# Three more items per tile in split precision, four of the differences on VectorE, and a new order of the engines' work

## The chip, the cores and the metric

The kernel runs on one core of a Trainium2 chip. The metric is the device time of one execution in microseconds (us). The median of three runs of the kernel before is 1046.57 us (1046.28 to 1047.83).

## The reference

The reference is a recommendation tower. Per sample 32 rows of 16 numbers are looked up (one in each of 32 tables), three cross layers follow, and then a small dense network. Batch 1024.

```python
e = jnp.stack([tbl_0[ids[:, 0]], ..., tbl_31[ids[:, 31]]], axis=1)        # (1024, 32, 16)
x0 = h = e
for i in range(3):                                  # W_i has 128 rows, b_i 128
    z = (x0[:, :, None, :] * h[:, None, :, :]).reshape(B, F * G, E)
    y = relu(einsum('oc,bce->boe', W[i], z) + b[i][None, :, None])
    x_keep, h = (y[:, :64], y[:, 64:]) if i != 2 else (y, y)
    xs.append(x_keep)
z = sum(concatenate(xs, axis=1), axis=2)            # (1024, 256)
h = maximum(concatenate([z, dense_ctx], axis=1) @ W_top1 + b_top1, 0)
h = maximum(h @ W_top2 + b_top2, 0)
y = h @ W_top3                                      # (1024, 1)
```

## The kernel before

A block is 128 samples, a tile is one block and 4 of the 16 embedding places: 512 columns. There are 8 blocks, so 32 tiles. A cross layer of a tile is a contraction over pairs of rows: VectorE multiplies a 128-row arrangement of x by h, two chunks of 128 pairs at a time (128x1024 numbers), and TensorE multiplies the chunks by the weights and adds up in PSUM. Such a pair of chunks is an **item**, written (layer, number): (0,0) and (0,1), (1,0) to (1,7), (2,0) to (2,7). Layer 0 has one more, smaller piece, the squares, called TAIL.

An item is multiplied in one of two ways. **Whole**: the product `prod` and the weights are plain fp32, two matmuls. **Split**: ScalarE rounds the product to fp32r (`high`), another engine makes the rest, `unsplit - high` (`low`), and TensorE does three fp32r matmuls per chunk: high by the weights' high part, high by their low part, and low by the high part. Before, 7 of the 8 items of layer 2 are split, 11 items are whole. GpSimd (POOL in the profile) makes all 7 differences, except three in the last slot.

The work is written out by hand as **slots**. Slot s holds layer 0 of tile s+1, layer 1 of tile s and layer 2 of tile s-1; the list `SLOT` gives the items' order, and every engine walks through it and waits on semaphores. Slots go from -1 to 32; those from 2 to 29 are in a loop of four slots. TensorE does the low part of a split item one item later than its high part. Products lie in rings: four for whole items, four for items that POOL finishes, two for VectorE's. A ring's buffer comes free when TensorE has finished the item in it (`s_used`).

Around the items stand, on each engine, in its own order:

- POOL issues the lookups of the next block, eight per slot (each an indirect DMA of 128 rows), and the tail's difference (`split_tail`). The lists `LOOKUPS_AFTER` place them between the differences.
- ScalarE casts `high`, makes h of the next layer from the PSUM sums (`next_h0`, and for h1 at a slot's end), copies the kept halves to SBUF (`keep`), copies the looked-up block into `emb` once per block (`take_rows`, which waits until all 32 lookups have landed), spreads it (`repeat_fields`), and takes the transposed x (`take_x`: a copy that goes to HBM and comes back in two arrangements, and the squares).
- VectorE makes the products, adds the kept halves of a tile to `acc_kept` (`add_kept`), the last layer to `acc_last` (`add_last`), and once per block sums the four places (`fold`).
- SyncE (SP) stores x and loads its arrangements `shifted` (1 MB) and `spread` (four loads of 1 MB) for each tile.

PSUM's eight banks before: y0, y1, two y2, two h0, h1, xT.

Of the kernel before, what the change touches and what calls it, by code (L numbers as in the profile page):

```python
# [30 lines left out]
ALU = mybir.AluOpType  # L31
# [7 lines left out]
P = 128  # L39
# [32 lines left out]
def uses_of_parity(t):  # L72
# [7 lines left out]
SLOT = [(1, 0), (1, 1), (2, 0), (1, 2), (2, 1), (1, 3), (0, 0), (2, 2), TAIL, (1, 4), (0, 1),  # L80
        (2, 3), (1, 5), (2, 4), (1, 6), (2, 5), (1, 7), (2, 6), (2, 7)]
# [3 lines left out]
TURN_AFTER = {-1: (0, 1), 0: (1, 4)}  # L85
# [45 lines left out]
class Plan:  # L133
# [28 lines left out]

    def place(self, s, item, ring):

        kind = self.kind(s, item)
        if isinstance(s[0], int):
            return self.entry(s, item) % ring[kind]
        return (self.before(kind, s[1]) + self.rank(s, item)) % ring[kind]


def dlrm_tower(nc, dense_ctx, ids, tables, w_top1, b_top1, w_top2, b_top2, w_top3,
# [8 lines left out]
    with ExitStack() as ctx:  # L180
# [98 lines left out]
        y2 = [ps(f"y2_{p}", [P, COLS]) for p in range(2)]  # L279
        h0 = [ps(f"h0_{p}", [P, COLS]) for p in range(2)]  # L280
# [3 lines left out]
        prep = [bank[:, :].rearrange("p (a b) -> p a b", b=P) for bank in y2]  # L284
# [50 lines left out]
        s_sum_kept = sem("s_sum_kept")  # L335
# [940 lines left out]
```

## Time and profile before

| | |
|---|---|
| median of 3 runs | 1046.57 us |
| the profiled execution | 1047.29 us |
| its span, first to last instruction | 1045.5 us |
| mean granted TensorE clock | 0.99 |
| busy: TensorE, VectorE, ScalarE, GpSimd | 96%, 74%, 47%, 78% |

The span is 1.8 us shorter than the time of the same execution. Each engine's busy time is a share of the span. A matmul's end is modelled, so what an item costs TensorE is read from where the next one starts, not from its own length.

### The profile page before, as it was taken

To read this page: it belongs to the slowest core of one execution; us is meant where nothing else is said; L and a number is where in the kernel's file an instruction comes from. 1 tells how busy PE (TensorE), PEld (TensorE's weight loads), DVE (VectorE), ACT (ScalarE), POOL (GpSimd) and SP (SyncE) were. 2 spreads that over 40 slices of the span, in tenths; PEclk is the share of its full clock that TensorE was granted. 3 is DMA by queue.
4 is the path that set the end of the run, shared out by engine and by line. 5 is a ranking of instruction groups with operands and counts; after the bars stand their busy time and mean duration, and the time that the engine had idled before them with its cause. 6 is when DMAs were issued, how large, how long until landed. Compare 5 with 4: busy or idle time off the path is not lost.

```text
span 1045.5 us, 11551 instructions
## 1 busy us (share of the span) xinstructions
PE 1007.8 (96%) x3261; PEld 590.5 (56%) x3261; DVE 771.7 (74%) x723; ACT 491.7 (47%) x630; POOL 813.8 (78%) x524
## 2 busy tenths in 40 slices
PE   3889999999999999999999999999999999999988
PEld 3744555555555555555555555555555555555555
DVE  4356787778787777777788777777788777777982
ACT  2153554544444554544444554454444555453443
POOL 6666889887989789887989789888989855556640
PEclk9899999999999999999999999999999999999999
DMA  8099998888998888888898888888897878779000
GB/s 160 8 203 219 204 201 180 180 182 178 198 200 174 189 176 183 181 181 179 193 203 171 192 177 184 181 180 181 190 204 167 198 176 181 177 179 218 16 1 1
DMA packets 42868, 176.27 MB, mean 169 GB/s; under 512 B 15522, under 2 KB 20130, under 8 KB 22372
## 3 DMA queue, kind: packets, MB, share of 16 engines
q1 hardware_dynamic: 34660, 173.96, 75.3%
q0 software_dynamic: 8192, 2.11, 1.9%
q8 instruction: 8, 0.13, 0.1%
q14 instruction: 8, 0.07, 0.0%
HBM read 172.89 MB, written 3.15 MB: 168 GB/s over the span
## 4 chain that ended last, share of the span: by engine, by line
PE 82%; DVE 5%; POOL 3%; DMA 3%; issue 2%; ACT 2%; SPq 2%; POOLq 0%; ACTq 0%; DVEq 0%
PE y L640 51%; PE y L648 17%; PE y L663 9%; POOL low L509 2%; PE xT L600 2%; DVE unsplit L1107 1%; PE xT L612 1%; DMA spread<-xcols 1%; DVE prod L1107 1%; POOL looked_up L499 1%; DMA looked_up<-in_tbl,ids_now 1%; SPq L431 1%; PE y L657 1%; DMA xcols<-xrows 1%; DVE z_kept_low L1184 0%
## 5 line engine op out<-in xcount | busy, mean ns | idle before, releaser
L509 POOL TENSOR_TENSOR low<-unsplit,high 128x1024 fp32r<-128x1024 f32 x221 | 525.1, 2389 | 120.9 <-ACT high L866 118.6
L640 PE MATMUL y<-prod,w1T 128*128 128x512 f32 x1024 | 477.8, 594 | 3.2 <-ACT kept L858 2.1
L1107 DVE TENSOR_TENSOR prod<-spread,h 128x1024 f32<-128x1024 f32 x288 | 349.6, 1216 | 122.4 <-PE y L640 105.4
L866 ACT CAST high<-unsplit 128x1024 fp32r<-128x1024 f32 x224 | 233.9, 1045 | 267.1 <-DVE unsplit L1107 266.9
L1107 DVE TENSOR_TENSOR unsplit<-spread,h 128x1024 f32<-128x1024 f32 x224 | 271.8, 1214 | 84.6 <-ACT h L852 84.6
L499 POOL DMA_INDIRECT looked_up<-in_tbl,ids_now x256 | 246.5, 963 | 66.1 <-issue 56.9
L640 PEld LDWEIGHTS y<-prod,w1T 128*128 128x128 f32 x1024 | 192.4, 190 | 162.5 <-issue 141.2
L648 PE MATMUL y<-high,w2T_high 128*128 128x512 f32 x448 | 226.7, 506 | 4.3 <-ACT high L866 4.3
L663 PE MATMUL y<-low,w2T_high 128*128 128x512 f32 x448 | 202.4, 533 | 2.3 <-POOL low L509 2.0
L648 PE MATMUL y<-high,w2T_low 128*128 128x512 f32 x448 | 177.5, 396 | 0.0
L852 ACT ACTIVATE h<-y,bias 64x512 f32<-64x512 f32 x128 | 83.3, 651 | 169.9 <-PE y L640 169.0
L663 PEld LDWEIGHTS y<-low,w2T_high 128*128 128x128 f32 x448 | 84.3, 190 | 85.7 <-issue 61.5
L640 PE MATMUL y<-prod,w0T 128*128 128x512 f32 x256 | 122.0, 599 | 3.1 <-DVE prod L1107 3.1
L648 PEld LDWEIGHTS y<-high,w2T_high 128*128 128x128 f32 x448 | 84.8, 189 | 49.5 <-issue 29.9
L648 PEld LDWEIGHTS y<-high,w2T_low 128*128 128x128 f32 x448 | 84.7, 189 | 43.5 <-issue 29.2
L1107 DVE TENSOR_TENSOR prod<-shifted,xT 128x1024 f32<-128x1024 f32 x64 | 77.8, 1216 | 16.5 <-DMA shifted<-xcols 6.5
L640 PEld LDWEIGHTS y<-prod,w0T 128*128 128x128 f32 x256 | 48.9, 192 | 46.9 <-issue 41.3
L640 PE MATMUL y<-prod,w2T_whole 128*128 128x512 f32 x128 | 60.1, 592 | 0.0
L517 POOL TENSOR_TENSOR tail_parts<-tail,tail_high 128x512 fp32r<-128x512 f32 x32 | 41.2, 1287 | 4.7 <-ACT tail L846 4.7
L858 ACT ACTIVATE kept<-y,bias_kept 64x512 f32<-64x512 f32 x64 | 43.7, 682 | 1.6
L841 ACT COPY xrows<-xT 48x512 f32<-48x512 f32 x32 | 18.5, 578 | 46.4 <-PE xT L612 46.3
L833 ACT COPY four_times<-emb 128x512 f32<-128x512 f32 x32 | 35.2, 1099 | 0.8
(117 smaller groups left out, 427.6 us busy)
## 6 DMA issues: line engine op xcount, KB each, us to landing
spread<-xcols SPq DMA_DIRECT2D x128, 1024.0 KB, 9.7
shifted<-xcols SPq DMA_DIRECT2D x120, 256.0 KB
looked_up<-in_tbl,ids_now POOLq DMA_INDIRECT x256
xcols<-xrows SPq DMA_DIRECT2D x32, 96.0 KB, 2.0
spread<-in_L_rec_W SPq DMA_DIRECT2D x3, 512.0 KB, 6.7
spread<-in_L_rec_W SPq DMA_DIRECT2D x1, 1024.0 KB, 11.2
wt<-in_W_top SPq DMA_DIRECT2D x2, 512.0 KB, 8.2
spread<-in_L_rec_W SPq DMA_DIRECT2D x2, 224.0 KB, 9.0
```

The costliest lines, as they stand in the source:

```text
L499: pool.indirect_dma_start(out=looked_up[:, f, :], out_offset=None, in_=tables[f][:, :], in_offset=bass.IndirectOffsetOnAxis(ap=ids_now[:, ...
L509: pool.tensor_tensor(low[kind][r][:, :, :], unsplit[kind][r][:, :, :], high[kind][r][:, :, :].bitcast(F32), ALU.subtract).then_inc(s_low[k ...
L517: pool.tensor_tensor(tail_parts[:, :], tail[:, :], tail_high[:, :].bitcast(F32), ALU.subtract).then_inc(s_tail_low, 1)
L600: pe.transpose(xT[:, 0:P], ident[:, :], ident[:, :])
L640: last = pe.matmul(y[:, :], w, z[:, c, :], start=(n == 0 and c == 0), stop=(item in (LAST0, LAST1) and c == ITEM - 1))
L648: pe.matmul(y[:, :], w[:, ITEM * n + c, :], z[:, c, :], start=(n == 0 and c == 0 and w is w2T_high), stop=False)
L663: last = pe.matmul(accumulator(s, layer)[:, :], w2T_high[:, ITEM * n + c, :], z[:, c, :], start=False, stop=(item == LAST2 and c == ITEM - 1))
L833: act.copy(four_times[:, :, :, :], emb[:, :, QUAD * q:QUAD * (q + 1)].rearrange("p f e -> p e f").unsqueeze(2).to_broadcast([P, QUAD, GROU ...
L852: last = act.activation(h[to, :], y[lanes, :], ACT.Relu, bias=bias[lanes, :])
L858: act.activation(kept[t[1] % KEPT][lanes, :], y[lanes, :], ACT.Relu, bias=bias_kept[lanes, :]).then_inc(s_kept, 1)
L866: act.copy(high[kind][r][:, :, :], unsplit[kind][r][:, :, :]).then_inc(s_high[kind], 1)
L1107: dve.tensor_tensor(z, x[:, ITEM * n:ITEM * (n + 1), :], b[:, :].unsqueeze(1).to_broadcast([P, ITEM, COLS]), ALU.mult).then_inc(s_made[kin ...
```

## The change

Ten items per tile are split instead of seven: all eight of layer 2, and (1,5) and (1,6) of layer 1, whose weights get a high and a low part in the preparation. VectorE makes the differences of four of them, (2,1), (1,5), (2,4), (2,6): it writes the product into a pair of PSUM banks (`pair`, one only), ScalarE casts from there, and VectorE subtracts from there, at the latest two products later (`LOW_BEHIND`). POOL has six differences instead of seven. To free the two banks there is now one y2 and one h0. The kept halves of a block's four tiles stay in SBUF and are summed by one reduction over 2048 columns per block (`sum_kept`); `add_kept` goes. The order of the items is new, and so is ScalarE's order around them: `take_rows` and `repeat_fields` stand at the start of a slot, the squares after (2,7), next_h0 after (1,7).

```diff
-SLOT = [(1, 0), (1, 1), (2, 0), (1, 2), (2, 1), (1, 3), (0, 0), (2, 2), TAIL, (1, 4), (0, 1),
-        (2, 3), (1, 5), (2, 4), (1, 6), (2, 5), (1, 7), (2, 6), (2, 7)]
+SLOT = [(1, 0), (1, 1), (1, 2), (1, 3), (2, 0), (2, 1), (2, 2), (2, 3), (1, 4), (1, 5), (0, 0),
+        TAIL, (0, 1), (2, 4), (2, 5), (1, 6), (1, 7), (2, 6), (2, 7)]
-WHOLE2 = (2, 6)
+BY_POOL_ITEMS = [(2, 0), (2, 2), (2, 3), (2, 5), (1, 6), (2, 7)]
+BY_DVE_ITEMS = [(2, 1), (1, 5), (2, 4), (2, 6)]
+FOUR_AFTER, X_AFTER, SQUARES_AFTER = None, (2, 5), (2, 7)
+H0_AFTER, H1_AFTER, KEPT0_AFTER, KEPT1_AFTER = (1, 7), (2, 7), (2, 3), (2, 7)
+SUM_KEPT_AFTER = (2, 3)
+LOW_BEHIND = 2
-LOOKUPS_AFTER = ((0, 0, 2, 0, 0, 3, 3), (0, 0, 1, 1, 1, 2, 2))
-LOOKUPS_FIRST = (0, 1)
+LOOKUPS_AFTER = ((0, 0, 3, 3, 0, 2),
+                 (0, 0, 4, 0, 1, 3))
...
             split_tail((0, -1))
-            for f in range(LOOKUPS_BEFORE_TAIL, FIELDS // TILES_PER_BLOCK):
+            for f in range(4, 8):
                 look_up(f)
-            split_tail((0, 0))
-            for f in range(FIELDS // TILES_PER_BLOCK, 3 * FIELDS // TILES_PER_BLOCK):
-                look_up(f)
+            early = of_kind(plan.items((0, 0)), BY_POOL)
+            for n in range(4):
+                if n < len(early):
+                    split_low((0, 0), early[n])
+                if n == 1:
+                    split_tail((0, 0))
+                for f in range(8 + 4 * n, 12 + 4 * n):
+                    look_up(f)
...
                 elif layer == 1:
-                    pe.wait_ge(s_kept1, number(s))
+                    if not isinstance(s[0], int) or number(s) >= 1:
+                        pe.wait_ge(s_h1, number(s))
+                        pe.wait_ge(s_kept1, number(s))
                 elif not isinstance(s[0], int) or number(s) >= 2:
-                    pe.wait_ge(s_sum2, number(s) - 2 + 1)
+                    pe.wait_ge(s_sum2, number(s) - 1 + 1)
...
+            def next_h0(s):
+                wait_for_layer(s, 0)
+                if LAST1 in plan.items(s):
+                    act.wait_ge(s_made[plan.kind(s, LAST1)], plan.entry(s, LAST1) + 1)
+                go_on(h0, y0, 1, bias0, s_h0)
+            def next_h1(s):
+                wait_for_layer(s, 1)
+                if LAST2 in plan.items(s):
+                    act.wait_ge(s_made[plan.kind(s, LAST2)], plan.entry(s, LAST2) + 1)
+                go_on(h1, y1, 0, bias1, s_h1)
             def slot(s):
...
+                if more and FOUR_AFTER is None:
+                    rows(nxt)
...
+                if kind == BY_DVE:
+                    if not isinstance(e, int) or e >= 1:
+                        dve.wait_ge(s_low[kind], e)
...
+            def sum_kept(t):
+                b = t[0] + t[1] // TILES_PER_BLOCK
+                dve.wait_ge(s_kept0, number(t) + 1)
+                dve.wait_ge(s_kept1, number(t) + 1)
+                dve.tensor_reduce(z_kept[:, bass.ds(P * b, P)],
+                                  kept[:, :, :].rearrange("p t c -> p (t c)").rearrange("p (e b) -> p b e", b=P),
+                                  AXIS.X, ALU.add).then_inc(s_z, 1)
```

**POOL in the first slots.** `tail_parts` is the tail's difference (of slot -1, then of slot 0), `looked_up` a lookup, `low...` an item's difference. Before:

```order
L499 DMA looked_up<-in_tbl_3,ids_now 128x16
L517 TENSOR_TENSOR tail_parts<-tail,tail_high 128x512 [waits s_tail_used,s_tail_high]
L499 DMA looked_up<-in_tbl_4,ids_now 128x16
L499 DMA looked_up<-in_tbl_5,ids_now 128x16
L499 DMA looked_up<-in_tbl_6,ids_now 128x16
L499 DMA looked_up<-in_tbl_7,ids_now 128x16
L517 TENSOR_TENSOR tail_parts<-tail,tail_high 128x512 [waits s_tail_used,s_tail_high]
L499 DMA looked_up<-in_tbl_8,ids_now 128x16
```

and now, where `low10_51` is the difference of slot 0's item (1,6):

```order
L518 DMA looked_up<-in_tbl_7,ids_now 128x16
L528 TENSOR_TENSOR low10_51<-unsplit0,high10 128x1024 [waits s_high1]
L518 DMA looked_up<-in_tbl_8,ids_now 128x16
L518 DMA looked_up<-in_tbl_9,ids_now 128x16
L518 DMA looked_up<-in_tbl_10,ids_now 128x16
L518 DMA looked_up<-in_tbl_11,ids_now 128x16
L537 TENSOR_TENSOR tail_parts<-tail,tail_high 128x512 [waits s_tail_used,s_tail_high]
L518 DMA looked_up<-in_tbl_12,ids_now 128x16
```

The difference of (1,6) and four lookups now stand ahead of slot 0's tail. TensorE still does the tail in the middle of slot 0, ahead of (0,1), (1,4), (1,5) and (1,6).

**ScalarE at the start of the slot in which a new block's rows are taken** (the loop's first slot, s = 2, 6, 10, ...; `emb<-looked_up` is `take_rows`, `four_times<-emb` is `repeat_fields`, the casts are those of the split items). Before:

```order
L866 CAST high13<-unsplit13 128x1024 [waits s_made1]
L864 REGISTER_ALU
L866 CAST high10<-unsplit10 128x1024 [waits s_made1]
L864 REGISTER_ALU
L866 CAST high11<-unsplit11 128x1024 [waits s_made1]
L824 ISA
L825 COPY emb<-looked_up 128x512 [waits s_looked]
L832 ISA [waits s_emb]
L833 COPY four_times<-emb 128x512 [waits s_xT]
```

and now:

```order
L858 COPY emb<-looked_up 128x512 [waits s_looked]
L865 ISA [waits s_emb]
L866 COPY four_times<-emb 128x512 [waits s_xT]
L901 ISA
L906 CAST high13<-unsplit3 128x1024 [waits s_made1]
L901 ISA
L904 REGISTER_ALU [waits s_made2]
L906 CAST high21<-pair 128x1024 [waits s_used2]
```

The wait for the lookups stood behind the casts of (2,0), (2,1) and (2,2); now it is the slot's first instruction, ahead of the cast of (2,0).

**POOL in the same slot, behind the tail's difference** (`ids_now` is the list of the next block's rows). Before:

```order
L486 COPY ids_now<-ids_sb 128x32
L488 REGISTER_ALU
L499 DMA looked_up<-in_tbl_0,ids_now 128x16 [waits s_now]
L499 DMA looked_up<-in_tbl_1,ids_now 128x16
L507 REGISTER_ALU
L509 TENSOR_TENSOR low12_51<-unsplit12,high12 128x1024 [waits s_high1]
L507 REGISTER_ALU
L509 TENSOR_TENSOR low13_52<-unsplit13,high13 128x1024 [waits s_high1]
L507 REGISTER_ALU
L509 TENSOR_TENSOR low10_49<-unsplit10,high10 128x1024 [waits s_high1]
L499 DMA looked_up<-in_tbl_2,ids_now 128x16
```

and now (`low12_53` is (2,5), `low13_54` is (1,6), `low10_51` is (2,7)):

```order
L518 DMA looked_up<-in_tbl_0,ids_now 128x16 [waits s_now]
L518 DMA looked_up<-in_tbl_1,ids_now 128x16
L518 DMA looked_up<-in_tbl_2,ids_now 128x16
L526 REGISTER_ALU
L528 TENSOR_TENSOR low12_53<-unsplit2,high12 128x1024 [waits s_high1]
L518 DMA looked_up<-in_tbl_3,ids_now 128x16
L518 DMA looked_up<-in_tbl_4,ids_now 128x16
L518 DMA looked_up<-in_tbl_5,ids_now 128x16
L526 REGISTER_ALU
L528 TENSOR_TENSOR low13_54<-unsplit3,high13 128x1024 [waits s_high1]
L526 REGISTER_ALU
L528 TENSOR_TENSOR low10_51<-unsplit0,high10 128x1024 [waits s_high1]
```

Six lookups instead of two now stand ahead of the slot's last differences.

## Rows read from the trace of the kernel before

**Rows 1.** The page: busy us, share, instructions; SP's DMA queue: packets, MB, share.
```profile
PE 1007.8 (96%) x3261; PEld 590.5 (56%) x3261; DVE 771.7 (74%) x723; ACT 491.7 (47%) x630; POOL 813.8 (78%) x524
...
q1 hardware_dynamic: 34660, 173.96, 75.3%
```
**Rows 2.** Timeline of TensorE: start us, us, engine line op out<-in xcount.
```profile
500.06 3.60 PE L640 MATMUL y<-prod,w1T 128*128 128x512 f32 x8
...
512.43 0.63 PE L663 MATMUL y<-low,w2T_high 128*128 128x512 f32 x2
512.89 1.88 PE L640 MATMUL y<-prod,w1T 128*128 128x512 f32 x4
...
969.44 3.17 PE L640 MATMUL y<-prod,w1T 128*128 128x512 f32 x7
```
**Rows 3.** Chain that ended last, in order of time: start us, us, what.
```profile
959.84 0.93 PE y L648 x4
960.76 1.72 PE y L640 x4
...
994.39 3.39 DVE unsplit L1107 x3
```
**Rows 4.** Timeline of TensorE, the first slots.
```profile
55.10 3.49 PE L640 MATMUL y<-prod,w0T 128*128 128x512 f32 x4 [2.93 <-DVE prod L1107]
...
71.95 0.80 PE L657 MATMUL y<-tail_parts,w0T_tail 128*128 128x512 f32 x1
...
84.64 5.40 PE L640 MATMUL y<-prod,w1T 128*128 128x512 f32 x8 [2.11 <-ACT kept L858]
```
**Rows 5.** Timeline of VectorE, the first slots.
```profile
77.56 2.35 DVE L1107 TENSOR_TENSOR prod<-spread,h 128x1024 f32<-128x1024 f32 x2 [3.17 <-DMA spread<-xcols]
```
**Rows 6.** Timeline of POOL: the first slots, then steady state.
```profile
64.85 1.27 POOL L517 TENSOR_TENSOR tail_parts<-tail,tail_high 128x512 fp32r<-128x512 f32 x1 [4.70 <-ACT tail L846]
...
78.77 0.94 POOL L499 DMA_INDIRECT looked_up<-in_tbl,ids_now  x1 [0.30 <-issue]
...
246.73 0.99 POOL L499 DMA_INDIRECT looked_up<-in_tbl,ids_now  x1 [0.82 <-POOL ids_now L486]
...
503.65 7.08 POOL L509 TENSOR_TENSOR low<-unsplit,high 128x1024 fp32r<-128x1024 f32 x3
510.68 1.28 POOL L517 TENSOR_TENSOR tail_parts<-tail,tail_high 128x512 fp32r<-128x512 f32 x1
```
**Rows 7.** Timeline of ScalarE, steady state.
```profile
516.76 1.31 ACT L852 ACTIVATE h<-y,bias 64x512 f32<-64x512 f32 x2 [3.80 <-PE y L640]
518.10 0.68 ACT L858 ACTIVATE kept<-y,bias_kept 64x512 f32<-64x512 f32 x1
```
**Rows 8.** Groups of instructions by line (the page's part 5).
```profile
L866 ACT CAST high<-unsplit 128x1024 fp32r<-128x1024 f32 x224 | 233.9, 1045 | 267.1 <-DVE unsplit L1107 266.9
```
**Rows 9.** Groups by line: a block's sum, and the tile's sum of layer 2.
```profile
L1151 DVE SCALAR_TENSOR_TENSOR acc_last<-y,neg_last,acc_last 128x512 f32<-128x512 f32 x24 | 17.8, 742 | 0.8 <-PE y L663 0.8
L1157 DVE TENSOR_REDUCE z_kept<-acc_kept 128x512 f32 x7 | 7.4, 1051 | 0.0
```
**Rows 10.** Timeline, POOL and ScalarE: the last lookup of two blocks, and its use.
```profile
44.80 0.94 POOL L499 DMA_INDIRECT looked_up<-in_tbl,ids_now  x1 [0.30 <-issue]
...
47.28 0.62 ACT L825 COPY emb<-looked_up 128x512 f32<-128x512 f32 x1 [22.51 <-DMA looked_up<-in_tbl,ids_now]
...
235.00 0.94 POOL L499 DMA_INDIRECT looked_up<-in_tbl,ids_now  x1 [0.30 <-issue]
...
243.18 0.62 ACT L825 COPY emb<-looked_up 128x512 f32<-128x512 f32 x1 [1.15 <-DMA looked_up<-in_tbl,ids_now]
```
**Rows 11.** Windows: us, busy of PE, PEld, DVE, ACT, POOL, PEclk, DMA share, GB/s.
```profile
55.00:59.00 4.00, 3.90 (x6) 1.89 (x7) 2.87 (x7) 0.63 (x1) 3.14 (x4) 0.60 0.97 228
235.00:237.00 2.00, 2.00 (x8) 1.30 (x8) 2.00 (x3) 1.05 (x1) 1.48 (x2) 1.00 0.99 205
```
**Rows 12.** Timeline of VectorE, the last slot.
```profile
997.77 3.02 DVE L1115 TENSOR_TENSOR low<-unsplit,high 128x1024 fp32r<-128x1024 f32 x1
```

More of the change, by code:

```diff
@@ L161, in entry, with finisher @@
         return TILES_PER_BLOCK * self.steady[kind] * s[0] + self.before(kind, s[1]) + self.rank(s, item)
+    def finisher(self, s, layer):
+        ends, waiting = [], None
+        for item in self.items(s):
+            if item != TAIL and self.kind(s, item) == WHOLE:
+                ends.append(item)
+            if waiting:
+                ends.append(waiting)
+            waiting = item if item == TAIL or self.kind(s, item) != WHOLE else None
+        if waiting:
+            ends.append(waiting)
+        return [item for item in ends if item[0] == layer][-1]
     def place(self, s, item, ring):
@@ L661, in multiply_low @@
                 pe.wait_ge(s_low[kind], plan.entry(s, item) + 1)
+                w_high, of = (w1T_high[item], 0) if layer == 1 else (w2T_high, ITEM * n)
                 for c in range(ITEM):
-                    last = pe.matmul(accumulator(s, layer)[:, :], w2T_high[:, ITEM * n + c, :],
-                                     z[:, c, :], start=False, stop=(item == LAST2 and c == ITEM - 1))
+                    last = pe.matmul(accumulator(s, layer)[:, :], w_high[:, of + c, :],
+                                     z[:, c, :], start=False,
+                                     stop=(item == plan.finisher(s, layer) and c == ITEM - 1))
                 last.then_inc(s_used[kind], 1)
@@ L669, in slot @@
                 nxt = after(s, 2)
-                turn_after = (2, 4) if (2, 4) in items else TURN_AFTER.get(number(s))
+                turn_after = EARLY_TURN_AFTER[number(s)] if isinstance(s[0], int) and number(s) < 1 else TURN_AFTER
                 waiting = None
@@ new lines, in keep1, with first_slots @@
+            def keep1(s):
+                wait_for_layer(s, 1)
+                keep(s, y1, 1, s_kept1)
+            def first_slots(n):
+                s = (0, n)
+                for item in plan.items(s):
+                    if n == 0 and item == (1, 0):
+                        keep0(s)
+                    if item != TAIL and plan.kind(s, item) != WHOLE:
+                        split_high(s, item)
+                    if item == (0, 0):
+                        repeat_fields(after(s, 2))
+                next_h0(s)
+                take_x(after(s, 2))
+                take_squares(after(s, 2))
+                if n == 0:
+                    next_h1(s)
+                    keep1(s)
```

279 lines of the change are left out of this document (149 added, 130 removed).

## The prediction

> **What bounds the kernel now.** I read the busy shares first: TensorE is busy 96% of the span, POOL 78%, VectorE 74%, ScalarE 47% [rows 1]. The reader should see one engine at its limit and three with room. Then TensorE's timeline: slot 15 starts at 500.06, slot 31 at 969.44, so a slot lasts 469.38/16 = 29.34 us [rows 2]. It is matmuls end to end: a whole item takes 1.72, the four high matmuls of a split item 0.93 [rows 3], its low pair 12.89 - 12.43 = 0.46 [rows 2]. 11 x 1.72 + 7 x 1.39 = 28.65, and the tail (0.23) and x's transposes (0.44) make 29.3. So between about 90 and 994 us only TensorE's work counts. The two ends are different: TensorE starts slot 1 at 84.64 [rows 4], and in slot 32 VectorE leads the chain [rows 3].
>
> **Splitting three more items.** 1.72 - 1.39 = 0.33 each, 0.98 per slot; a slot becomes 28.36 us, if nothing else is late. 31 slots (1 to 31) give **-30.3 us**.
>
> **VectorE.** 18 products and four differences at 3.39/3 = 1.13 [rows 3] make 24.9, one addition for the last layer 0.74 [rows 9], a quarter of two block sums about 0.9: 26.5 us in a slot of 28.4. A difference that reads PSUM is not in the trace at this place; as a two-input operation on 1024 columns with one operand in PSUM it is priced like the product. The only row of a difference from SBUF beside POOL's has 3.02 [rows 12]; that end would give 34 us per slot. I take 1.13, since the products run beside POOL too, from one PSUM operand. The new block sum reads 2048 columns where the old one read 512 in 1.05 us [rows 9]: between 1.05 (it writes the same 128) and 4.2 (four times). Over a plain 512-column operation (0.74) the old sum costs 0.3 more, and 2048 columns at the products' rate are 2.3, so I take 2.6. At 2.6 VectorE catches up in the next wait; at 4.2 it makes (2,7) late enough to hold TensorE 0.6 us per block. I count **+1** for all of it. The adds of kept halves go, off the path.
>
> **TensorE's waits inside a slot.** I count from the slot's start. (1,0) needs y1 copied out: layer 1's last matmul (the low of (1,6)) ends at 25.6; then 0.2, h1 1.31 and the kept half 0.68 [rows 7] end at 27.8, before 28.4. h0 waits for the tail's matmul at 19.7: h0 is there at 21.2. The casts of (2,6) and (2,7) stand behind it on ScalarE, 1.0 each [rows 8]: 23.2, in time for 26.5. The squares (1.6) follow until 24.8, before h1 can start. y2 is single: slot s's (2,0) at 6.9 needs the sum of the tile before, which VectorE has at about 2.7. So an ordinary slot holds, with 0.5 to 1 us to spare. POOL: six differences of 2.36 (7.08/3) with the tail 1.28 and eight lookups of 0.94 + 0.30 [rows 6] are 25.4 of 28.4.
>
> **The first slots.** Before, POOL does slot 0's tail at 64.85, long before TensorE wants it at 71.95 [rows 4, 6]. Now it stands behind the difference of (1,6). VectorE can make (1,6) only when the fourth part of spread has landed, at 77.56 [rows 5], and the change leaves that load where it is. So: product 78.8, cast 79.9, difference 82.4, four lookups 87.4, tail 88.7. TensorE is idle from 72 to 88.7. After an idle stretch it restarts at half speed: after 2.93 us idle an item took 3.49 instead of 1.72, with the granted clock at 0.60 over those 4 us [rows 4, 11] (1.2 GHz most of the time, then 2.4). So 0.23 + 1.72 + 1.75 bring (0,1) to 92.4, then (1,4), transposes, (1,5), (1,6) and (1,7) with their lows, 6.7: 99.1. h1 and the kept half: 101.3 against 84.64 for slot 1: +16.7. Before, slots 1 to 14 lose 500.06 - 14 x 29.34 - 84.64 = 4.7 us; 1.8 is the restart, which stays, and 2.9 are other waits while POOL is behind, which I let go, since TensorE is late for all of them. Net **+13.8 us**.
>
> **Once per block: the lookups.** This is the term I am least sure of. In the slot ahead of a new block's rows (s = 1, 5, ...) POOL's last three lookups follow the difference of (2,7): cast ends 23.2, difference 25.7, lookups start at 25.8, 27.1 and 28.35, that is at the next slot's 0. When do they land? The very first block's last lookup is used 47.28 - 44.80 = 2.5 us after its start; in steady state it takes 243.18 - 235.00 = 8.2, with the DMA engines at 0.99 [rows 10, 11]. Both are bounds here: 2.5 to 8.2. The loads of a tile keep the DMA engines for 0.753 x 1045.5/32 = 24.6 us [rows 1] of 28.4, and by my count the last of the slot drains about 2 us into the next one. I take 3.0. ScalarE now waits for it ahead of everything: rows 0.7, fields 1.0, cast of (2,0) 1.0, so POOL's first difference starts at 5.8. Ahead of the end of (1,6)'s difference POOL has three differences 7.1, tail 1.3, the ids and their gap 1.0, six lookups 7.5 and two more differences 4.8: 21.7, ready at 27.5. TensorE wants it at 25.1. It waits 2.4, and restarts slowly at a cost between 0 (idle 0.5 us) and 1.8 (idle 2.1, at 84.64, where eight matmuls took 5.40 instead of 3.60 [rows 2, 4]); I take 1.2. That is 3.6 in each of slots 6, 10, 14, 18, 22: **+18 us**. In slot 2 the loads are behind from the start: between 3.6 and 9, I take **+6**. In slot 26 no lookups follow, only ScalarE's lateness: **+1**.
>
> The row says 2.5 or 8.2 us for one and the same lookup, by load. The Trainium skill ("DMA: Bandwidth & Descriptors", section on the anatomy of one DMA on the GpSimd path) gives such a DMA about 2.0 us plus its bytes at 436 GB/s. By that rule the rows land at about 2.0 and the block costs 1.4 us of waiting without a restart, an estimate of 7 us for the five blocks in place of 18. The same page (section on queues, rings and completion order) lets a DMA engine take turns between queues a packet at a time, which would fit the 8.2.
>
> **The end.** In slot 31 VectorE has 16 products, four differences, and four parts of the dense layers' weights and sums (6.6 us), together about 30 us where TensorE has 24 (no layer 0), with a lead of a few us to use up: +3. In slot 32 the difference (3.02 us, [rows 12]) and the additions of kept halves from SBUF give way to PSUM reads and one sum: -2.5, though one y2 puts the sum ahead of TensorE's first matmul there. Net **+0.5**.
>
> **Sum.** 1045.5 - 30.3 + 13.8 + 1 + 18 + 6 + 1 + 0.5 = 1055.5 us of span. The profiled execution took 1.8 more than its span (1047.29), and the median lies 0.7 below that: **1056.6**; I say 1056.
>
> **Rivals.** *A, on the other side, faster: the block's lookups land in time or nearly so.* Place: ScalarE's first instruction in slots 2, 6, ... Price: at 2.5 us landing TensorE waits 1.9, too short to slow it; if SP's loads drain before the slot ends and POOL is ahead, nothing. The sum is 1045.5 - 30.3 + 13.8 + 5 x 0 to 1.9 + 3 + 0.5 = 1032.5 to 1042, or 1033 to 1043 by the median. It decides at a landing of about 0.7 us into the slot for no wait, and of 2.6 for a wait with no restart. For it: the 2.5 of the first block. Against: lookups start only at the slot's 0, and every steady block shows 8. *B: the loads leave no gap*, and the three lookups wait behind them for 8.2 or more. TensorE waits 7.6 and restarts: 9.4 in five blocks, 9 in slot 2, 4 in slot 26: 1045.5 - 30.3 + 13.8 + 1 + 47 + 9 + 4 + 0.5 = 1090.5, 1091 by the median. For it: all seven later blocks. Against: there the lookups were issued while four loads were just beginning. *C: VectorE binds*, because each of its four hand-overs through the one pair (product, cast, difference) leaves it bare for 0.8 us: 26.5 + 3.2 = 29.7 per slot, 1.3 over TensorE's, 40 us in all, which takes the place of the block's waits: 1045.5 + 13.8 + 10 + 0.5 + 6 = 1076. Against: my walk finds only one such wait, at (2,6). *D: the head does not slip* because POOL gets there sooner: -14, 1042. The order of POOL's instructions and the landing at 77.56 leave little for it.
>
> **Chances.** The forecast 0.45, A 0.25, B 0.15, C 0.10, D 0.05. Range 1032 to 1088: it holds the forecast, A, C and D; above it lies most of B. The likeliest case alone is 1048 to 1066. What a measurement of this kernel can tell from no change is about 0.2%, 2.1 us: faster is below 1044.5. Faster: A and D, 0.28. Same: the low end of the forecast, 0.07. Slower: 0.65.
>
> **What the profile after would show.** Steady slots 28.4 us apart, apart from one in four, which is some 3 us longer, with TensorE waiting for POOL's difference ahead of the low matmuls of (1,6), and ScalarE idle before `emb`, released by the lookups. TensorE idle from 72 to about 88.7 with slot 0's tail the releaser, and slot 1 at about 101. The block's sum at 2.6 us, VectorE's differences at 1.2. Wrong would be: every slot longer than 28.6, TensorE waiting for VectorE, or no wait in the fourth slots.

## The result and the profile after

| | before | after |
|---|---|---|
| median | 1046.68 us (4 runs) | 1091.67 us (4 runs, 1091.1 to 1094.23) |
| the profiled execution, its span | 1047.29, 1045.5 | 1091.1, 1089.3 |
| mean granted TensorE clock | 0.99 | 0.973 |

The ratio is 1.0428, with an interval of 1.0416 to 1.044: slower by 4.3%. The forecast was 1056 with a range up to 1088. The time of rival B, 1091, is what came; how much of that is luck stands in the section on why the prediction was wrong.

The page of the changed kernel, to be held against [rows 1] (busy us, share, instructions; SP's DMA queue; the chain by engine):

```profile
PE 998.0 (92%) x3453; PEld 631.5 (58%) x3453; DVE 900.9 (83%) x819; ACT 587.3 (54%) x726; POOL 743.6 (68%) x495
...
q1 hardware_dynamic: 34660, 173.96, 73.1%
...
POOL 47%; issue 30%; PE 12%; DVE 6%; DMA 3%; ACT 2%; POOLq 0%; SPq 0%; ACTq 0%; DVEq 0%
```

The chain by engine in the kernel before:

```profile
PE 82%; DVE 5%; POOL 3%; DMA 3%; issue 2%; ACT 2%; SPq 2%; POOLq 0%; ACTq 0%; DVEq 0%
```

TensorE fell from 96% to 92% of a span that is longer, and POOL's share of the chain rose from 3% to 47%. The bytes are the same. TensorE's timeline, first slots and then the starts of slots 5, 6 and 7, answers to [rows 2, 4]:

```profile
86.73 0.80 PE L686 MATMUL y<-tail_parts,w0T_tail 128*128 128x512 f32 x1 [15.03 <-POOL tail_parts L537]
...
99.99 1.53 PE L668 MATMUL y<-prod,w1T 128*128 128x512 f32 x3 [2.16 <-ACT h L889]
...
221.30 1.12 PE L668 MATMUL y<-prod,w1T 128*128 128x512 f32 x2
...
249.84 7.03 PE L668 MATMUL y<-prod,w1T 128*128 128x512 f32 x16
260.43 0.50 PE L677 MATMUL y<-high,w2T_high 128*128 128x512 f32 x1 [3.56 <-ACT high L906]
...
281.71 0.72 PE L694 MATMUL y<-low,w1T_high 128*128 128x512 f32 x2 [1.01 <-POOL low L528]
...
285.08 1.45 PE L668 MATMUL y<-prod,w1T 128*128 128x512 f32 x3
```

An ordinary slot lasts 28.43 us (29.34 before), slot 5 lasts 249.84 - 221.30 = 28.54, and slot 6, the first with a new block's rows, 285.08 - 249.84 = 35.24. Over 28.43 the seven such slots (2, 6, ..., 26) lose 5.4, 6.8, 7.35, 8.3, 6.6, 14.7 and 6.3, together 55.5 us.

The whole difference in the start of slot 31, 969.44 before [rows 2] and 1012.24 after, is 42.8: +15.35 at slot 1, +55.5 in the seven slots, +2 in slot 1 (30.39 us long, by short waits; the granted clock was 1.00 all through it), +2.2 in the slots in which a block's sum stands and the ones behind them (28.64 and 28.54), less 0.4 in slot 30 (28.01), less 30 x 0.91 = 27.3 for the split, and less 4.6 that before lost between slots 1 and 15. From slot 31 on, 77.1 us against 76.1.

What happens in slot 6 shows on ScalarE (the end of slot 5 and `take_rows`) and on POOL, which answer to [rows 7, 10]:

```profile
248.57 0.69 ACT L895 ACTIVATE kept<-y,bias_kept 64x512 f32<-64x512 f32 x1
257.66 0.62 ACT L858 COPY emb<-looked_up 128x512 f32<-128x512 f32 x1 [8.40 <-DMA looked_up<-in_tbl,ids_now]
258.38 1.05 ACT L866 COPY four_times<-emb 128x512 f32<-128x512 f32 x1
259.34 1.04 ACT L906 CAST high<-unsplit 128x1024 fp32r<-128x1024 f32 x1
```
```profile
249.94 0.94 POOL L518 DMA_INDIRECT looked_up<-in_tbl,ids_now  x1 [0.30 <-issue]
260.45 2.39 POOL L528 TENSOR_TENSOR low<-unsplit,high 128x1024 fp32r<-128x1024 f32 x1 [9.57 <-ACT high L906]
```

The last lookup starts at 249.94 and its rows are taken at 257.66: 7.7 us, not 3.0. ScalarE does nothing for 8.4 us, and (2,0), cast at 259.34, is late for TensorE, which has done layer 1's first four items. The wait of 3.56 us is followed, 1.5 us later, by 3.4 us of matmuls at the lower clock (granted 0.50 below, that is 1.2 GHz). The two waits, 3.56 and 1.01, are 4.6 of slot 6's 6.8; the lower clock is about 1.7 more, an estimate (half of 3.4). Why the landing took so long shows in SP's timeline (store of x, loads of `shifted`, four loads of `spread`) and in the windows:

```profile
238.13 0.36 SPq L415 DMA_DIRECT2D xcols<-xrows  x1
245.37 1.82 SPq L421 DMA_DIRECT2D shifted<-xcols  x4
247.48 23.96 SPq L433 DMA_DIRECT2D spread<-xcols  x4
```
Windows: us, busy of PE, PEld, DVE, ACT, POOL, PEclk, DMA share, GB/s.
```profile
245.00:246.00 1.00, 1.00 (x4) 0.42 (x3) 1.00 (x2) 0.99 (x3) 1.00 (x1) 1.00 0.00 0
246.00:247.00 1.00, 1.00 (x4) 0.57 (x3) 1.00 (x2) 0.53 (x1) 1.00 (x1) 1.00 0.74 238
264.00:265.00 1.00, 1.00 (x4) 0.81 (x3) 1.00 (x2) 0.00 (x0) 1.00 (x1) 0.50 1.14 238
265.00:266.00 1.00, 1.00 (x5) 0.76 (x5) 1.00 (x2) 0.95 (x1) 1.00 (x2) 0.83 0.10 16
270.00:271.00 1.00, 1.00 (x8) 0.83 (x7) 1.00 (x2) 0.90 (x2) 0.74 (x1) 1.00 0.00 0
```

The DMA engines do have free time in each slot, but it lies at 265 to 271, 15 to 21 us into the slot. `shifted` and three loads of `spread`, 4 MB in one stretch, go out once x has been stored, 4.5 us before the slot's end, and run for 19 us across the place where the lookups are awaited. The fourth load of `spread` in the row above goes out only at 270.89, since in `load_spread` it waits for the product of (2,5).

Other prices, by group (busy, mean ns, idle before): VectorE's differences and the block's sum, against [rows 9, 12].

```profile
L1220 DVE TENSOR_TENSOR low<-pair,high 128x1024 fp32r<-128x1024 f32 x128 | 156.2, 1220 | 86.9 <-ACT high L906 86.9
L1253 DVE TENSOR_REDUCE z_kept<-kept 128x2048 f32 x7 | 26.9, 3839 | 0.0
```

And two places that the prediction didn't have: POOL and TensorE at the end of slot 22, and TensorE in the last slot.

```profile
765.50 0.94 POOL L518 DMA_INDIRECT looked_up<-in_tbl,ids_now  x1 [8.06 <-issue]
```
```profile
768.87 1.22 PE L694 MATMUL y<-low,w2T_high 128*128 128x512 f32 x2 [5.09 <-POOL low L528]
...
1042.46 0.79 PE L677 MATMUL y<-high,w2T_high 128*128 128x512 f32 x1 [3.65 <-DVE acc_last L1245]
```

### The profile page after: what moved, and what is told of

Same layout as the page of the kernel before. It is cut to its first block, busy times and chain, and to the rows that moved or that the text cites. A ratio compares the mean times of both kernels' runs of the same rounds, so it can differ in the third digit from the quotient of the medians.

```text
span 1089.3 us, 12275 instructions
## 1 busy us (share of the span) xinstructions
PE 998.0 (92%) x3453; PEld 631.5 (58%) x3453; DVE 900.9 (83%) x819; ACT 587.3 (54%) x726; POOL 743.6 (68%) x495
## 3 DMA queue, kind: packets, MB, share of 16 engines
HBM read 172.89 MB, written 3.15 MB: 162 GB/s over the span
## 4 chain that ended last, share of the span: by engine, by line
POOL 47%; issue 30%; PE 12%; DVE 6%; DMA 3%; ACT 2%; POOLq 0%; SPq 0%; ACTq 0%; DVEq 0%
POOL low L528 24%; POOL looked_up L518 20%; PE y L668 5%; PE y L677 3%; POOL tail_parts L537 3%; PE y L694 2%; DVE unsplit L1212 2%; DVE prod L1212 1%; DMA spread<-xcols 1%; DMA looked_up<-in_tbl,ids_now 1%; DVE pair L1212 1%; ACT high L906 1%; DVE low L1220 1%; DVE z_kept L1253 0%; ACT hidden_high L1027 0%
## 5 line engine op out<-in xcount | busy, mean ns | idle before, releaser
L528 POOL TENSOR_TENSOR low<-unsplit,high 128x1024 fp32r<-128x1024 f32 x192 | 455.7, 2389 | 228.3 <-ACT high L906 227.3
L668 PE MATMUL y<-prod,w1T 128*128 128x512 f32 x768 | 348.4, 596 | 4.5 <-ACT h L889 2.2
L1212 DVE TENSOR_TENSOR prod<-spread,h 128x1024 f32<-128x1024 f32 x192 | 225.2, 1213 | 34.1 <-DMA spread<-xcols 15.2
L1212 DVE TENSOR_TENSOR unsplit<-spread,h 128x1024 f32<-128x1024 f32 x192 | 228.5, 1214 | 10.3 <-ACT h L889 7.9
L668 PEld LDWEIGHTS y<-prod,w1T 128*128 128x128 f32 x768 | 145.7, 191 | 156.2 <-issue 139.5
L906 ACT CAST high<-unsplit 128x1024 fp32r<-128x1024 f32 x192 | 200.3, 1047 | 55.0 <-DVE unsplit L1212 48.7
L1220 DVE TENSOR_TENSOR low<-pair,high 128x1024 fp32r<-128x1024 f32 x128 | 156.2, 1220 | 86.9 <-ACT high L906 86.9
L906 ACT CAST high<-pair 128x1024 fp32r<-128x1024 f32 x128 | 129.9, 1015 | 174.9 <-DVE pair L1212 169.7
L1212 DVE TENSOR_TENSOR pair<-spread,h 128x1024 f32<-128x1024 f32 x128 | 156.7, 1225 | 1.1
L694 PE MATMUL y<-low,w1T_high 128*128 128x512 f32 x128 | 63.3, 575 | 8.2 <-POOL low L528 8.0
```

The source lines that it names most:

```text
L528: pool.tensor_tensor(low[kind][r][:, :, :], unsplit[r][:, :, :], high[kind][r][:, :, :].bitcast(F32), ALU.subtract).then_inc(s_low[kind], 1)
L668: last = pe.matmul(y[:, :], w, z[:, c, :], start=(n == 0 and c == 0), stop=(item == plan.finisher(s, layer) and c == ITEM - 1))
L694: last = pe.matmul(accumulator(s, layer)[:, :], w_high[:, of + c, :], z[:, c, :], start=False, stop=(item == plan.finisher(s, layer) and c ...
L906: act.copy(high[kind][r][:, :, :], source[:, :, :]).then_inc(s_high[kind], 1)
L1212: dve.tensor_tensor(z, x[:, ITEM * n:ITEM * (n + 1), :], b[:, :].unsqueeze(1).to_broadcast([P, ITEM, COLS]), ALU.mult).then_inc(s_made[kin ...
L1220: dve.tensor_tensor(low[kind][r][:, :, :], pair[:, :, :], high[kind][r][:, :, :].bitcast(F32), ALU.subtract).then_inc(s_low[kind], 1)
```

## The experiments

All are edits of the changed kernel. Each ratio is to runs of the kernel before that were taken beside it; their medians lie between 1047.0 and 1047.7 us. "Less" without another base means less than the changed kernel.

### Slot 0's tail first on POOL

```diff
             early = of_kind(plan.items((0, 0)), BY_POOL)
+            split_tail((0, 0))
             for n in range(4):
                 if n < len(early):
                     split_low((0, 0), early[n])
-                if n == 1:
-                    split_tail((0, 0))
```

> The changed kernel, with slot 0's tail difference on POOL back ahead of the difference of (1,6) and its four lookups. Theory 1 (the 15 us idle of TensorE at 72 to 87 us is POOL's order, and POOL's backlog comes next): TensorE no longer waits at the tail and slot 1 starts at about 84 instead of 100 us, but 16 lookups (20 us) still stand behind the difference of (1,6), which is ready at 82, so slot 1's difference of (2,0) comes at about 104 where TensorE wants it at 94: it waits 10 us there. Net about -6 us: 1086. Rival (the order of the tail is all there is to it): -15 us, 1076. Rival 2 (the loads set the head anyway): no change, 1092.

Measured: 1085.15 us, ratio 1.0349 (1.0332 to 1.0367), 6.5 less than the changed kernel. TensorE's timeline:

```profile
83.86 3.67 PE L667 MATMUL y<-prod,w1T 128*128 128x512 f32 x8 [2.16 <-ACT h L888]
...
102.28 1.22 PE L693 MATMUL y<-low,w2T_high 128*128 128x512 f32 x2 [8.14 <-POOL low L528]
```

Slot 1 starts 16 us earlier, where it was before. But 16 lookups stand ahead of slot 1's first difference, and TensorE waits 8.14 us for that. This is what theory 1 said, 6 less at 1086. The tail's place made the wait; POOL's lookups decide how much of it comes back.

### The difference of (1,6) behind ten lookups

```diff
+            split_tail((0, 0))
+            for f in range(8, 18):
+                look_up(f)
+            for item in early:
+                split_low((0, 0), item)
+            for f in range(18, 24):
+                look_up(f)
```

This stands in place of the loop of four.

> The changed kernel with POOL's order in slot 0 rewritten: slot 0's tail, ten lookups, then the difference of (1,6), then six lookups. Putting the tail first alone gave 1085.2 and not 1076, because the difference of (1,6) with lookups behind it then made slot 1's (2,0) wait 8.1 us for its low part. Theory 1 (the whole head loss of 15.35 us is POOL's order in the first slots): slot 1 starts at 84 to 85, no wait of more than 3 us behind it, slot 2 at about 116; time 1075 to 1078. Rival (POOL's sum of work up to slot 2 is what binds, whatever the order): the wait turns up at another difference, and the time stays at 1083 to 1086.

Measured: 1078.15 us, ratio 1.0289 (1.0269 to 1.0308): 13.5 less. Slot 1 starts at 84.25 and slot 2 at 116.79, with no wait above 2.2 us in slot 1. POOL issues the ten lookups in the time in which it would only wait for the cast of (1,6); its wait for that cast was 18.07 us in the changed kernel and is 0.41 now. So theory 1 holds: the head's loss is the order of POOL's work.

### The rows taken behind (2,3)

```diff
-FOUR_AFTER, X_AFTER, SQUARES_AFTER = None, (2, 5), (2, 7)
+FOUR_AFTER, X_AFTER, SQUARES_AFTER = (2, 3), (2, 5), (2, 7)
```

> The changed kernel, with ScalarE's take_rows and repeat_fields behind the cast of (2,3) instead of at the slot's start. Theory (once per block ScalarE, waiting for the lookups ahead of the cast of (2,0), holds TensorE, and POOL's differences then come late a second time): the slots 2, 6, ..., 26, which are 33.8 to 43.1 us long, become 28.5: -50 to -56 us, 1036 to 1042. Rival (POOL's six lookups ahead of the last differences of these slots are what costs, whenever ScalarE comes): about 1 to 2 us per block stay, 1045 to 1052. Rival 2 (the wait moves to the cast of (1,5)): less than half of it comes back.

Measured: 1042.4 us, ratio 0.9942 (0.9925 to 0.9959): 49.3 less than the changed kernel, from one constant; theory 1 said 50 to 56. Slot 6 now starts at 247.84 and slot 7 at 276.29, 28.45 later:

```profile
247.84 7.03 PE L668 MATMUL y<-prod,w1T 128*128 128x512 f32 x16
...
276.29 7.03 PE L668 MATMUL y<-prod,w1T 128*128 128x512 f32 x16
```

ScalarE still waits for the lookups:

```profile
255.37 0.62 ACT L858 COPY emb<-looked_up 128x512 f32<-128x512 f32 x1 [0.94 <-DMA looked_up<-in_tbl,ids_now]
```

The last lookup started at 247.95, 7.4 us earlier. The landing is as slow as ever; no cast stands behind it that TensorE wants soon. Slot 22 still lasts 32.81 us, with its third lookup 4.43 us late.

### All eight lookups of a later slot at once

In the other three slots of a block the eight lookups all stand behind the tail's difference.

```diff
-                 (0, 0, 4, 0, 1, 3))
+                 (0, 0, 8, 0, 0, 0))
```

> The changed kernel, with all eight lookups of the slots with quarter 1 to 3 behind the tail's difference, none behind (1,6) and (2,7); ScalarE's order as in the change. Theory (what counts is how late the last lookup is issued): it is issued about 9 us earlier and has landed when the slot ends, ScalarE does not wait, slots 2, 6, ... become about 28.5; POOL's difference of (1,6) is 0.2 to 1 us late in the other three slots of a block. Net -45 to -55 us with up to +15: 1037 to 1062. Rival (ScalarE's wait is for something else, or lookups under load always take as long as they need until the loads pause): -10 us or less.

Measured: 1053.03 us, ratio 1.0052 (1.0036 to 1.0069), 38.6 less. With the last lookup 8.5 us ahead of `emb`, ScalarE no longer waits for it in any block but the first. It is 10.6 above the rows-late kernel. A part of that shows: four lookups more now stand ahead of (2,5)'s difference, and TensorE waits 0.8 us for it in most blocks, and 3.15 in slot 8, behind a lookup that comes 3.94 us late. The two profiled executions are only 4.0 apart (1048.77, the fastest of this kernel, and 1044.73, the slowest of the other), so the profiles don't account for all of the 10.6.

```profile
240.81 0.73 PE L694 MATMUL y<-low,w2T_high 128*128 128x512 f32 x2 [0.80 <-POOL low L528]
```

### A quarter of the fourth load

`load_spread(..., 3)` loads one of its four chunks, 0.25 MB instead of 1 MB; part of the input is left out. Nothing else is touched, neither POOL's nor ScalarE's order.

```diff
+                some = 1 if g == GROUPS - 1 and not (isinstance(t[0], int) and number(t) < 2) else GROUP
...
-                                     [[2 * COLS, P // RUN], [0, RUN], [1, GROUP * COLS]])
+                                     [[2 * COLS, P // RUN], [0, RUN], [1, some * COLS]])
```

> The changed kernel, where of the fourth part of spread (chunks 12 to 15) only chunk 12 is loaded from tile 2 on: 256 KB instead of 1 MB, same number of instructions and semaphores; it leaves out part of the input. Theory (the last lookups take 7.7 us because a tile's big loads still run; they were held up because the store of x queued behind the third load of spread): the loads drain about 3.6 us earlier, the lookups land at about 4 us instead of 7.7 after their issue, and a block's long slot is 3 to 4 us shorter: -20 to -27 us, 1065 to 1072. Rival (a lookup takes about 8 us in steady state by itself): no change of the landing, 1090 to 1092.

Measured: 1058.43 us, ratio 1.01 (1.0084 to 1.0117), 33.2 less, and below what was expected. ScalarE and POOL at slot 6's start (250.02):

```profile
252.77 0.62 ACT L859 COPY emb<-looked_up 128x512 f32<-128x512 f32 x1 [3.34 <-DMA looked_up<-in_tbl,ids_now]
```
```profile
250.12 0.94 POOL L519 DMA_INDIRECT looked_up<-in_tbl,ids_now  x1 [0.30 <-issue]
255.61 2.38 POOL L529 TENSOR_TENSOR low<-unsplit,high 128x1024 fp32r<-128x1024 f32 x1 [4.55 <-ACT high L907]
```

```profile
276.88 0.73 PE L695 MATMUL y<-low,w1T_high 128*128 128x512 f32 x2 [1.53 <-POOL low L529]
```

The loads stop at 251.3 and go on at 253.2. Between the two, the same lookup lands in 2.65 us instead of 7.7, and slot 6 loses 1.8 us over 28.43 instead of 6.8. The number of lookups is the same, so it is the loads that hold them. The run also shows the case that I forecast: with a landing of 2.65, TensorE's only wait above 0.3 us in slot 6 is 1.53 us at the low matmuls of (1,6), for POOL. That is the place that I named. A block costs 1.8 there, where I had 2.4 and a restart of 1.2 at 3.0.

### The store of x ahead of the third load

SP's order in each tile: the store of x, then the third load of `spread` of the tile before, which stood ahead of it.

```diff
                 store_x(t)
+                load_spread(after(t, -1), GROUPS - 2)
                 load_shifted(t)
                 load_spread(after(t, -1), GROUPS - 1)
-                for g in range(GROUPS - 1):
+                for g in range(GROUPS - 2):
                     load_spread(t, g)
```

> The changed kernel; in SP's order the store of x and spread's third load (1 MB) change places, so that the store goes out first. Nothing else. In the changed kernel the load is issued at 236.5, the store at 238.1, the loads of shifted, which wait for the store to land, only at 245.4, and the DMA engines stand nearly idle for some 1.5 us before that. Theory 1 (the store queues behind the load, and this delays the rest of the tile's loads and with them the block's last lookups): shifted issued about 2 us after the store, the hole goes, the last lookup lands 1.5 to 4 us earlier (5 instead of 7.7 after its start), each block's start costs 2 to 4 us less: 1091.7 less 12 to 25 = 1067 to 1080. Rival (the loads are limited by the buffers that come free late in the new order, and the hole is only taken from later): the lookups land as before, 1089 to 1093.

Measured: 1086.5 us, ratio 1.0373 (1.0357 to 1.0389): 5.2 less, a fifth to two fifths of what theory 1 wanted, and below the rival's 1089 to 1093. ScalarE, POOL and SP ahead of slot 6 (255.08), and two windows:

```profile
262.39 0.62 ACT L860 COPY emb<-looked_up 128x512 f32<-128x512 f32 x1 [7.89 <-DMA looked_up<-in_tbl,ids_now]
```
```profile
255.19 0.94 POOL L520 DMA_INDIRECT looked_up<-in_tbl,ids_now  x1 [0.30 <-issue]
```
```profile
244.03 0.59 SPq L433 DMA_DIRECT2D spread<-xcols  x1
246.43 1.82 SPq L421 DMA_DIRECT2D shifted<-xcols  x4
```
```profile
269.00:270.00 1.00, 1.00 (x5) 0.82 (x4) 1.00 (x2) 0.22 (x1) 1.00 (x2) 0.72 0.65 131
270.00:271.00 1.00, 1.00 (x6) 0.81 (x5) 1.00 (x2) 0.80 (x1) 1.00 (x1) 1.00 0.01 0
```

`shifted` does go out 3 us after the store instead of 7.2, and 8.65 us ahead of the slot's end instead of 4.5. The landing is 7.2 instead of 7.7. But the third load, which now follows the store, has joined the stretch: it is 5 MB long instead of 4. It ends at 269.7, 14.6 us into the slot, where it ended 15.3 us into it (265.1 with the slot's start at 249.84). So it covers the lookups as before. The store's place in the queue is a small part of the cause. The stretch's length and the point at which x is taken are left for the rest; no run changes the second.

### Head and rows together, and three more edits on top

The base is the second and the third edit in one kernel.

> The edit above and the one that puts the taking of the block's rows behind (2,3) on ScalarE, in one kernel. Theory 1 (the two losses, 15 us in the head and some 7 per block, are independent): 1042.4 (rows late alone) less 15 = 1027 (1025 to 1031), and slots of 28.4 us everywhere. Rival (POOL's and VectorE's backlog of the first slots is only made up by TensorE's waits, so the head's gain is given back in the first blocks): 1034 to 1040.

Measured: 1028.88 us, ratio 0.9817 (0.9803 to 0.9831). The two gains add up (13.5 + 49.3 = 62.8 off 1091.7 is 1028.9). From slot 3 to slot 30 only slot 22 still has a wait of TensorE above 0.3 us, here on POOL and TensorE:

```profile
706.91 0.94 POOL L518 DMA_INDIRECT looked_up<-in_tbl,ids_now  x1 [4.32 <-issue]
```
```profile
716.34 1.22 PE L694 MATMUL y<-low,w1T_high 128*128 128x512 f32 x2 [2.54 <-POOL low L528]
```

**The last slot.** The base with `add_last` ahead of `sum_kept`, by exchanging the two `if`s for (2,0) of the last slot.

> The kernel before this one (head and rows), and in the last slot VectorE adds the last layer's sum ahead of the block's sum of 3.8 us. Theory 1 (TensorE's wait of 3.65 us at 1042 in the changed kernel is the block's sum standing ahead of that addition): 3 to 4 us less than without the swap, about 1024. Rival (VectorE leads the last slot, and only the order of its work changes): no difference within 1 us.

Measured: 1029.25 us, ratio 0.9824 (0.981 to 0.9838). No difference: the rival.

```profile
977.06 0.50 PE L677 MATMUL y<-high,w2T_high 128*128 128x512 f32 x1 [0.84 <-DVE acc_last L1245]
...
982.85 0.80 PE L677 MATMUL y<-high,w2T_high 128*128 128x512 f32 x1 [4.32 <-ACT high L906]
```

The wait of 3.65 for `acc_last` becomes 0.84, and 4.32 turn up six microseconds later, for the cast of a product that now stands behind the block's sum.

**Nine split items.** The base with (1,6) whole and off POOL's list.

```diff
-BY_POOL_ITEMS = [(2, 0), (2, 2), (2, 3), (2, 5), (1, 6), (2, 7)]
+BY_POOL_ITEMS = [(2, 0), (2, 2), (2, 3), (2, 5), (2, 7)]
-SPLIT1 = [(1, 5), (1, 6)]
+SPLIT1 = [(1, 5)]
-LOOKUPS_AFTER = ((0, 0, 3, 3, 0, 2),
-                 (0, 0, 4, 0, 1, 3))
+LOOKUPS_AFTER = ((0, 0, 3, 3, 2),
+                 (0, 0, 4, 1, 3))
```

> Head and rows, with item (1,6) whole instead of split: nine split items, five differences on POOL. Theory 1 (TensorE alone bounds an ordinary slot, an item that is split saves 0.33 us): a slot lasts 28.43 + 0.33 = 28.76, 31 slots cost 10 us, time 1036 to 1039. Rival (POOL or VectorE sets the pace in some slots, so the third split item brings less than it promises): 1027 to 1033.

Measured: 1028.69 us, ratio 0.9824 (0.9804 to 0.9844): the same as with ten. Slots 10 and 11 start at

```profile
346.79 0.59 PE L668 MATMUL y<-prod,w1T 128*128 128x512 f32 x1
```
```profile
375.52 1.88 PE L668 MATMUL y<-prod,w1T 128*128 128x512 f32 x4
```

28.73 apart. By TensorE's work theory 1 was right: 0.31 more than 28.43. But all slots are alike here, while with ten items they average 28.52 (28.43 and 28.45, then 28.64 and 28.54 where the block's sum stands and behind it), and slot 22 waits for POOL. The tenth split item gives 0.22 per slot, 6 us, and that is given back in slot 22 (4.2), in the first slots (0.8 at slot 2's start) and behind slot 31's start (0.9). By the time the rival was right, by the slot's length theory 1.

**Slot 22's lookup.** The base with a block's first eight lookups placed otherwise between POOL's differences:

```diff
-LOOKUPS_AFTER = ((0, 0, 3, 3, 0, 2),
+LOOKUPS_AFTER = ((0, 0, 2, 0, 4, 2),
```

> Head and rows late (1028.9), and in the first slot of a block POOL's eight lookups stand as two behind (2,3)'s difference, four behind (1,6)'s and two behind (2,7)'s, instead of three, three, none and two. In every version of the changed kernel the third lookup of slot 22 is issued 4 to 8 us late, with the difference of (1,6) behind it, and TensorE waits 2.5 us or more for that. Theory 1 (that late lookup is the whole of slot 22's loss, and it comes at the same lookup wherever it stands): the third lookup is late again, now behind the differences of (2,5) and (1,6), TensorE's wait there goes, slot 22 lasts 28.5 us instead of 32: 1028.9 less 3 to 4 = 1025 to 1026. Rival (the stall hits whatever stands at that time, or (2,7)'s difference is now late instead): 1028 to 1030.

Measured: 1023.86 us, ratio 0.9777 (0.9764 to 0.979), the best of all: 2.2% faster than before, and 5.0 less than the base. The page, and the third lookup of slot 22:

```profile
PE 978.3 (96%) x3453; PEld 622.6 (61%) x3453; DVE 899.8 (88%) x819; ACT 588.0 (58%) x726; POOL 745.2 (73%) x495
```
```profile
708.20 0.96 POOL L518 DMA_INDIRECT looked_up<-in_tbl,ids_now  x1
```

The time is 1.1 below what theory 1 said, slot 22 lasts 28.45, and the reason is another: the lookup isn't late at all. Why it isn't stays open. In slot 8 one still is, by 4.41 us, where POOL has the time. Behind slot 2's start and up to the last two slots TensorE has no wait above 0.5 us.

### Everything, and the store ahead

The base with the last slot's exchange and the store of x ahead of the third load.

> Head, rows late, the last slot's swap and the store ahead, all in one. With the rows taken late, no slot but the 22nd waits for lookups or loads any more (1029.3 without the store's move). Theory 1 (with the rows late the landing of the lookups is off the path): the same within 2 us, 1027 to 1031. Rival (the loads' earlier end also shortens POOL's stall of 4 to 5 us at slot 22's third lookup, or x's rows come earlier): 1024 to 1027.

Measured: 1029.81 us, ratio 0.983 (0.9817 to 0.9844), 0.6 from the same kernel without the store's move. Here nothing near the end of the chain waits for the loads, and their order is worth nothing.

## Why the prediction was wrong

**The step that failed** is "by my count the last of the slot drains about 2 us into the next one. I take 3.0". The last lookup lands 7.7 us after its start, not 3.0. The step rested on 24.6 us of transfers in a slot, and that is about right (0.731 x 1089.3/32 = 24.9); what was wrong is where in the slot the time without transfers lies. I put it at the slot's start, from 2 us on. It is behind the stretch of 4 MB that starts when x's columns have been stored, which `X_AFTER` puts late in the slot: in slot 6 it lies 15 to 21 us into it. I did have both ends, 2.5 and 8.2 [rows 10], and one line of "against" for rival B: that before, the lookups were issued while loads were just beginning. So they are now. In the kernel before, `shifted` went out 4.3 us ahead of the lookup of [rows 10] at 235.00:

```profile
230.75 1.82 SPq L402 DMA_DIRECT2D shifted<-xcols  x4
```

After, the two start at 245.37 and 249.94, 4.6 us apart. The row at 8.2 was a measurement of this very case. With 7.7 in place of 3.0, ScalarE's lateness first reaches TensorE at (2,0), not at (1,6) as in my sum. The quarter load, the late rows and the early lookups show the cause from three sides: 33, 49 and 39 us come back.

**What was luck.** Rival B's 1091 came only in part by its mechanism. B had the landing right (8.2 for 7.7), but not "the loads leave no gap": they leave 6 us in slot 6. It wanted 9.4 us in each of five slots, and four of the five lost 6.6 to 8.3. The sum is met because slot 22 lost 14.7, some 8 of it behind a lookup that came 8.06 us late, which neither the forecast nor a rival had. Without it the time would be about 1084, an estimate, inside my range, with the landing just as wrong.

**The rule and the row.** By the Trainium skill ("DMA: Bandwidth & Descriptors", section on the anatomy of one DMA on the GpSimd path) such a transfer takes some 2.0 us and its bytes. No run here has one as short; the nearest are 2.2 to 2.5 in the first block (2.5 in [rows 10], 2.24 in the changed kernel), and 2.4 to 3.0 behind the quarter load. Under loads it is 7.5 to 8.6 in slots 6 to 26 of the changed kernel. So the Trainium skill's 2.0 is near what a lookup takes with no loads beside it, and a quarter of what it takes here; the measurement decides.

**Point by point.**
- Ordinary slot: 28.36 forecast, 28.43 measured. The splitting is worth 0.91 per slot, where I had 0.98. Right.
- Head: slot 1 at 101.3 forecast, 99.99 measured; the tail at 88.7, measured 86.73. I let 2.9 us of later waits go and kept a restart of 1.8; in the accounting above, before lost 4.6 there and after 2, by short waits and without a restart. The net is +12.8 for my +13.8. Right, and undone by POOL's order alone (-13.5).
- VectorE: a difference from PSUM lasts 1.22, as long as a product (1.21), and that was my price. Rival C fell, though its hand-overs are there: 86.9/128 = 0.68 us each. In slot 6 of the kernel with head and rows together VectorE is busy for 25.1 us and idle for 2.6 ahead of the differences, 27.7 of 28.45, so there is little to spare. The block's sum was mis-sized: 3.84 against 2.6, near the upper bound of 4.2. The slot that holds it and the next one are 0.32 longer per block (28.64 - 28.43 and 28.54 - 28.43), which I put down to it untested: 2.2 in all for my +1.
- Once per block: +25 forecast (18, 6 and 1), 55.5 measured. Of these about 8 are slot 22's late lookup, which I didn't have. Rival B's sum for these slots was 60.
- The end: +0.5 forecast, +1.0 measured. The block's sum stands ahead of the last layer's there, and moving it gains nothing.
- The sum by the measured terms: 1045.5 - 27.3 + 15.35 + 55.5 + 2 + 2.2 - 0.4 - 4.6 + 1 = 1089.3, the measured span.
- The chances: I gave the forecast 0.45 and B 0.15. "Slower" at 0.65 was right. The range left most of B outside, although B had the only steady-state row for it.

**Open.** Why POOL's third lookup of slot 22 is issued 3 to 8 us late in the changed kernel and in ten of its eleven variants, why slot 8 has such a one in all of them, and why the kernel before has neither. The engine shows "issue", that is no wait that the profile knows. And by what way the loads hold a lookup (turns between the queues, or something else) no run tells.

## What to carry to other kernels

The average idle time on the DMA queues did not tell where in a slot it lay: lay the issue of each load over the slot, and take the latency of a small transfer from the row whose surroundings are the same, even where a shorter one is on hand. A wait that is moved ahead of other work in one engine's order delays all of that work; here the same kernel with that one wait put behind four casts was 4.5% faster. And a helper engine's order in the first slots deserves its own walk, since here the busiest engine's idle time there came back almost whole (13.5 us of 15).

## What the hardware showed

- The sum of 2048 strided columns took 3.84 us and that of 512 took 1.07, 1.9 and 2.1 ns a column; a product of 1024 columns took 1.21, 1.2 ns a column.
- A difference with one operand in PSUM took 1.22 us on VectorE. One from SBUF took 3.02 at 997.77 in the kernel before [rows 12], while POOL made its own differences from SBUF (one of these took 3.39 instead of 2.4). The next one from SBUF, with POOL idle, took 1.21:

```profile
1011.60 1.21 DVE L1115 TENSOR_TENSOR low<-unsplit,high 128x1024 fp32r<-128x1024 f32 x1
```

  So it is POOL beside it that goes with the 3.02, not SBUF alone. ScalarE's cast from PSUM took 1.015, from SBUF 1.047.
- The last lookup of a block (128 rows) landed in 2.65 us where the loads paused, and in 7.5 to 8.6 under 1 MB loads in slots 6 to 26 of the changed kernel (at 173 to 238 GB/s in the windows from 250 to 258).
- After 15.03 us of idle time TensorE ran at a granted clock of 0.50, here the windows around the tail, in slot 6 and twice in slot 14:

```profile
86.70:90.00 3.30, 3.27 (x5) 1.63 (x6) 0.00 (x0) 0.00 (x0) 2.56 (x3) 0.50 0.04 5
...
262.00:264.00 2.00, 2.00 (x6) 1.26 (x6) 2.00 (x3) 1.89 (x3) 2.00 (x2) 0.50 0.96 213
...
503.00:506.00 3.00, 2.76 (x12) 1.77 (x11) 2.41 (x3) 3.00 (x4) 3.00 (x2) 1.00 1.01 218
...
525.00:527.00 2.00, 2.00 (x6) 1.57 (x5) 0.91 (x1) 1.94 (x4) 1.84 (x2) 0.50 0.99 209
```

In slot 6 the idle time ahead was only 3.56 us, and matmuls at 262 to 265 still came 0.43 us apart instead of 0.23. But the length of the wait did not decide it. In slot 14 TensorE had waited 3.44 us at 502.57 and went on at a clock of 1.00; it had waited 2.14 us at 523.89, and there the clock fell to 0.50. So the prediction's choice of a restart by the wait's length (none at 1.9 us, a full one at 2.1) is not borne out: in slot 2 waits of 2.02 and 2.13 passed without one.
